# The order and the pacing of the indirect transfers that serve expert tiles beside an attention stage

## The reference

```python
xn = layernorm(x)
# attention
scores = einsum('bhqd,bhkd->bhqk', q, k) / sqrt(16) - slope[h] * |i - j|
s = (softmax(scores) @ v) @ W_out.T + b_out
# feed-forward: the 2 best of 8 experts per token, and a shared one
y = einsum('tei,eih->teh', silu(x @ w_gate) * (x @ w_up), w_down)
g = silu(einsum('teh,te->th', y, comb) + shared)
x = x + s * g
```

## Time and profile before

| | before |
|---|---|
| median of 3 runs | 1693.5 us (1691.61 to 1699.25) |
| profiled execution, its own time | 1699.23 us |
| span of its record | 1697.4 us, so 1.8 us lie around it |
| TensorE, ScalarE, VectorE, GpSimd busy | 90%, 78%, 60%, 29% of the span |
| granted clock of TensorE, mean | 0.975 of full speed |
| expert tiles on TensorE | from 496.0 us (first) to 1471.7 us (last turn) |

### The profile page before, as it was taken

One profiled execution on the slowest core, in us unless ns is written; L12 is line 12 of the kernel. 1 busy time (PEld: TensorE's weight loads), 2 busy tenths in 40 slices (PEclk: granted clock), 3 DMA queues, 4 the chain that ended last, 5 costly groups with the idle time before them and its releaser, 6 DMA issues. The chain is left out here.

```text
span 1697.4 us, 39816 instructions
## 1 busy us (share of the span) xinstructions
PE 1532.4 (90%) x15326; PEld 683.3 (40%) x15328; DVE 1012.4 (60%) x2738; ACT 1316.4 (78%) x1694; POOL 498.6 (29%) x477
## 2 busy tenths in 40 slices
PE   5998998889989999988999999989999999988896
PEld 3555564223334433333444333434443333322364
DVE  7788766988844444445444444454444444568776
ACT  5788777888878888877887878768888888788811
POOL 1222331000023333333443333333333333222143
PEclk9999998999999999999999999989999999999999
DMA  6858775233354454445454444445444454377795
GB/s 204 275 189 262 259 228 156 64 110 89 88 159 139 134 135 134 129 128 133 132 139 121 132 140 135 129 118 139 133 129 129 134 132 132 102 212 216 237 328 175
DMA packets 201087, 265.57 MB, mean 156 GB/s; under 512 B 90960, under 2 KB 158592, under 8 KB 200640
## 3 DMA queue, kind: packets, MB, share of 16 engines
q1 hardware_dynamic: 168256, 171.72, 36.1%
q0 software_dynamic: 24192, 82.86, 15.9%
q10 hardware_dynamic: 8448, 8.39, 1.4%
HBM read 180.56 MB, written 90.46 MB: 160 GB/s over the span
## 5 line engine op out<-in xcount | busy, mean ns | idle before, releaser
L1494 ACT ACTIVATE probs_att<-SC_att 128x1024 f32<-128x1024 f32 (+10 forms) x1306 | 1074.6, 912 | 209.3 <-PE SC_att L1377 179.5
L1403 PE MATMUL O_att<-probs_att,V_att 128*32 128x512 f32 (+7 forms) x8144 | 649.2, 414 | 61.1 <-DVE probs_att L1519 27.2
L1519 DVE TENSOR_TENSOR probs_att<-probs_att,decay 128x128 f32<-128x128 f32 x1024 | 265.7, 287 | 289.5 <-ACT probs_att L1494 246.9
L1403 PEld LDWEIGHTS O_att<-probs_att,V_att 128*32 128x32 f32 x8144 | 180.3, 111 | 221.0 <-issue 145.0
L1334 POOL DMA_INDIRECT ys<-ys_att,back_of_att x144 | 148.2, 1029 | 379.8 <-DVE ys_att L1585 272.1
L1377 PE MATMUL SC_att<-Q,K_turned_att 64*128 64x512 f16 (+7 forms) x1244 | 222.4, 310 | 15.7 <-ACT probs_att L1494 6.8
L1377 PE MATMUL SC_att<-Q,K 64*128 64x512 f16 (+9 forms) x1154 | 201.8, 303 | 10.3 <-DVE K_turned_att L1506 4.9
L1328 POOL DMA_INDIRECT x<-xn,row_of_att x144 | 139.5, 969 | 129.0 <-ACT probs_att L1494 98.2
L1322 POOL DMA_INDIRECT x<-w_rows,owner x72 | 74.0, 1028 | 346.8 <-DVE row_of_att L1568 215.2
L1377 PEld LDWEIGHTS SC_att<-Q,K_turned_att 64*128 64x128 f16 x1244 | 67.4, 94 | 266.3 <-ACT probs_att L1494 159.0
L699 POOL TENSOR_TENSOR inverse<-qk_tok,inverse 128x512 f16<-128x512 f32 x64 | 75.6, 1188 | 169.5 <-ACT inverse L731 162.6
(11 more groups left out here) (210 smaller groups left out, 1672.7 us busy)
## 6 DMA issues: line engine op xcount, KB each, us to landing
K<-k_stack SPq DMA_DIRECT2D x86, 256.0 KB
Q<-q_stack SPq DMA_DIRECT2D x86, 256.0 KB
x<-ys POOLq DMA_DIRECT2D x32, 512.0 KB, 4.8
x<-in_x SPq DMA_DIRECT2D x24, 512.0 KB, 7.2
k_stack<-inverse SPq DMA_DIRECT2D x96, 128.0 KB
q_stack<-inverse SPq DMA_DIRECT2D x96, 128.0 KB
inverse<-k_stack SPq DMA_DIRECT2D x42, 256.0 KB
inverse<-q_stack SPq DMA_DIRECT2D x42, 256.0 KB
```

The costliest lines, as they stand in the source:

```text
L1403: mm = pe.matmul(O[VW * g:VW * (g + 1), col:col + width * len(mine)], V[par][:, k, :], spans[:, j0:j0 + BPB * (len(mine) - 1) + 1:BPB, :], ...
L1494: nc.scalar.activation(probs[home][:, side + chunk.base:side + chunk.base + chunk.width], SC[:, c % SLOTS, start:start + chunk.width], ACT ...
L1519: v.tensor_tensor(diag, diag, decay[:, head_of(chunk.head), :], ALU.mult).then_inc(faded, 1)
```

## The change

The same 360 transfers (72 of weights, 144 of rows, 144 of results) are issued, with the same sizes, buffers and data semaphores. Two things differ.

The order: before, GpSimd goes through w(i+2), x0(i+2), x1(i+2), y0(i), y1(i) for each tile i. Now it goes through y0(i-1), x0(i+2), y1(i-1), x1(i+2), w(i+2). The results of a tile go out one tile later in the order, and the weights come last, not first.

The pace: before, the loads wait for 1500, 3300 and 5100 columns behind "turn" of tile i, the stores for 1500 and 3300 columns behind "down" of tile i. Now all five are counted from "turn" of tile i: 500, 2800, 5100, 7400 and 9700 columns, so 2300 apart. The last tile's results wait for no count. The first two tiles' loads are unpaced, as before.

```diff
-PACE_W, PACE_XS, PACE_YS = 1500, (3300, 5100), (1500, 3300)
+PACE_YS, PACE_XS, PACE_W = (500, 5100), (2800, 7400), 9700
...
-                def load_tile(i):
+                def load_weights(i):
                     if i > 2:
                         pool.wait_ge(ff_down, i - 2)
                     if i > 1:
                         pool.wait_ge(expd, after("turn", i - 2, PACE_W))
                     nc.gpsimd.indirect_dma_start(w[:, i % 3, :], ...)
+
+                def load_rows(i, t):
                     if i > 1:
                         pool.wait_ge(ff_turned, i - 1)
-                    for t in range(2):
-                        if i > 1:
-                            pool.wait_ge(expd, after("turn", i - 2, PACE_XS[t]))
-                        nc.gpsimd.indirect_dma_start(xs[:, i % 2, t, :], ...)
-
-                def store_tile(i):
+                        pool.wait_ge(expd, after("turn", i - 2, PACE_XS[t]))
+                    nc.gpsimd.indirect_dma_start(xs[:, i % 2, t, :], ...)
+
+                def store_rows(i, t):
                     pool.wait_ge(ff_y, i + 1)
-                    for t in range(2):
-                        pool.wait_ge(expd, after("down", i, PACE_YS[t]))
-                        nc.gpsimd.indirect_dma_start(keep["ys"], ...)
+                    if i + 1 < TILES_IN:
+                        pool.wait_ge(expd, after("turn", i + 1, PACE_YS[t]))
+                    nc.gpsimd.indirect_dma_start(keep["ys"], ...)
...
                 for i in range(TILES_IN):
+                    for t in range(2):
+                        if i > 0:
+                            store_rows(i - 1, t)
+                        if i + 2 < TILES_IN:
+                            load_rows(i + 2, t)
                     if i + 2 < TILES_IN:
-                        load_tile(i + 2)
-                    store_tile(i)
+                        load_weights(i + 2)
+                for t in range(2):
+                    store_rows(TILES_IN - 1, t)
```

More of the change, by code:

```diff
@@ L1322, in load_tile @@
                     nc.gpsimd.indirect_dma_start(w[:, i % 3, :], None, keep["w_rows"], index(keep["owner"][:, i:i + 1])).then_inc(w_in[i % 3], 16)
+                def load_rows(i, t):
                     if i > 1:
                         pool.wait_ge(ff_turned, i - 1)
-                    for t in range(2):
-                        if i > 1:
-                            pool.wait_ge(expd, after("turn", i - 2, PACE_XS[t]))
-                        nc.gpsimd.indirect_dma_start(xs[:, i % 2, t, :], None, keep["xn"], index(row_of[:, t, i:i + 1])).then_inc(xs_in[i % 2], 16)
-                def store_tile(i):
+                        pool.wait_ge(expd, after("turn", i - 2, PACE_XS[t]))
+                    nc.gpsimd.indirect_dma_start(xs[:, i % 2, t, :], None, keep["xn"], index(row_of[:, t, i:i + 1])).then_inc(xs_in[i % 2], 16)
+                def store_rows(i, t):
                     pool.wait_ge(ff_y, i + 1)
-                    for t in range(2):
-                        pool.wait_ge(expd, after("down", i, PACE_YS[t]))
-                        nc.gpsimd.indirect_dma_start(keep["ys"], index(back_of[:, t, i:i + 1]), ys[:, i % 2, t, :], None).then_inc(ys_out[i % 2], 16)
+                    if i + 1 < TILES_IN:
+                        pool.wait_ge(expd, after("turn", i + 1, PACE_YS[t]))
+                    nc.gpsimd.indirect_dma_start(keep["ys"], index(back_of[:, t, i:i + 1]), ys[:, i % 2, t, :], None).then_inc(ys_out[i % 2], 16)
                 def fetch(j):
@@ L1345, in _ @@
                 pool.wait_ge(order_ready, 1)
-                load_tile(0)
-                load_tile(1)
+                for i in range(2):
+                    load_weights(i)
+                    for t in range(2):
+                        load_rows(i, t)
                 for i in range(TILES_IN):
+                    for t in range(2):
[3 more added lines that the diff above has]
+                            load_rows(i + 2, t)
                     if i + 2 < TILES_IN:
-                        load_tile(i + 2)
-                    store_tile(i)
+                        load_weights(i + 2)
+                for t in range(2):
+                    store_rows(TILES_IN - 1, t)
                 for n in range(2):
```

## The result

The changed kernel took 1672.35 us in the median (1668.55 to 1676.03, 4 runs), the kernel before, beside it on the same chip, 1692.55 us (1687.52 to 1699.25, 4 runs). The ratio is 0.9887, with a 95% interval from 0.9863 to 0.9912.

The account below looks back on a forecast made before the run. TensorE (93% busy) and ScalarE, passing chunks through three PSUM slots, bound the tiles' stretch. All terms were 0, sum 0: 1693.5 us against the median; 8-in-10 range 1681 to 1702 us.

Parts of the forecast that it names:

- The moved loads and stores cost nothing: Tiles' stretch: moved transfers still land before turn, gate or result's copy needs them, 15.5 to 18.4 us to spare; worth 0.
- The narrowest margin: Narrowest case the plan allows, two tiles of 10,112 columns and a "down" 4,032 behind the turn: 9.7 us left.
- GpSimd's waits change from VectorE's to exponentials', at no cost: GpSimd's queue in the tiles' stretch: its 243.6 us of waiting for VectorE turn into waits for exponentials; worth 0.
- the end of the tiles stays: Behind the last tile: same copy releases the last store, fetch still leaves near 1484.8 us; worth 0.
- What the trace doesn't show ... I take 0: Tiles' stretch: whether an indirect transfer under way slows other engines; bounded from -31 to +35 us, taken as 0.
- a sign that the prediction itself named for being wrong: Tiles' stretch: TensorE's unexplained waits and its half-clock stretches cut to less than half, with a shorter time.
- The dismissal of the gap at 741 to 744 us: Longest TensorE gap, 3.45 us before 743.99: claimed TensorE partly at work with records missing, so weak support for bunches costing.
- first rival: Tiles' stretch: bunched loads keep DMA engines from something TensorE needs, so spreading gains; 1678 us, chance 0.16.
- Half of its bound: Size taken for bunches costing in the tiles' stretch: half of 31 us, giving 1678 us.
- The second rival: VectorE's fades and turning of K: GpSimd's spread issues hold them, up to 100 ns each; +18 us, 1711 us, chance 0.11.
- the 832 ns of K's turning: VectorE's longest turning of K, cited against GpSimd's issues holding VectorE, which would need one of over 1 us.
- It doesn't do what it says: GpSimd's issues: rounding to chunks brings transfers together again, so nothing changes, as in the forecast; no separate chance given.

Follow-up runs that it names:

- e2: Changed kernel, spacing still even, but weights issued first and the other transfers at other places in the tile; ratio 0.9893 to the kernel before.
- e4: Changed kernel's even spacing with the order of the kernel before (weights, rows, rows, result, result); ratio 0.9893 to the kernel before.
- e1: Changed kernel with all five counts at 5100 columns, so a tile's five transfers are issued back to back; 1796.23 us, ratio 1.0623 to before.
- e5: Bunched as e1, but each load moves only 64 bytes per partition, with the same number of issues; ratio 1.0676 to the kernel before.
- e8: Bunched as e1 with the same bytes, but loads are plain transfers from a fixed place, stores still indirect; ratio 0.9772 to the kernel before.
- e3: Changed kernel, still spread, but each load moves only 64 bytes per partition, with the same number of issues; ratio 0.9880 to the kernel before.
- e9: As e8, with the stores of 64 tiles made plain transfers to fixed places too; ratio 0.9752 to the kernel before.
- e10: As e8, with GpSimd filling each load's target with zeros ahead of the plain load; ratio 0.9770 to the kernel before.
- e11: As e1, with each indirect load fetching 64 rows instead of 128; ratio 1.0826 to the kernel before.

## Why the prediction was wrong, step by step

**The moved loads and stores cost nothing: right.** No wait before a turn, a gate or a result's copy was ended by a transfer, and e2 and e4 put the transfers elsewhere for the same time. (The narrowest margin, 9.7 us, leaves out the 3.7 us of TensorE's lead that the other three hold; it is 6.0.)

**GpSimd's waits change from VectorE's to exponentials', at no cost; the end of the tiles stays: right.** 198.7 us of waits before stores are for exponentials now, and behind the last tile the comparison by exponentials moves by 2 us only.

**"What the trace doesn't show ... I take 0": the step that failed.** The term was bounded from -31 to +35 us, and the measured -20 lies inside. I chose 0 because fades keep their median, "285 stands 14 ns from the minimum of 271". That row answers another question: how long an instruction takes once it has started. The fades' median is 285 ns in e1 too; what changes is when TensorE starts the next matmul and when a finished score reaches ScalarE. The rows for that were in the profile: ScalarE's waits for scores that had been done, and TensorE's 15.3 us without a recorded cause, whose fall to less than half, with a shorter time, is part of a sign that the prediction itself named for being wrong. The second of these rows needs care. At 743.99 TensorE starts 0.1 us behind the end of VectorE's copy (743.20 and 0.69 us), for which it waits; only the record of that signal is missing, and it was the copy that came late. Of all TensorE's waits of this kind between 505 and 1410 us, 21.2 us, 17.3 end within 0.16 us of the end of an instruction of VectorE or ScalarE. Most of them are time lost further down the chain, not holds of TensorE's own starts.

**The dismissal of the gap at 741 to 744 us: wrong.** "TensorE was at work in part of this gap and its records are missing" was the argument against the first rival. Every one of the 14 traces has 3560 score matmuls and 1306 exponentials, one for each chunk, and the page of the kernel before has 15326 matmuls beside 15328 weight loads, so by that count two matmuls are missing in the whole kernel. "Remote" says only that no recorded instruction ended shortly before the semaphore rose. VectorE's copy waits there for a semaphore that TensorE's sums raise, and the last of them ended, as modelled, at 738.49, 4.7 us before. TensorE stood, right behind four indirect issues in a row.

**The first rival: right on the gain, wrong on the cause.** Half of its bound gave 1678 us; 1672 came out. The half was chosen and not worked out, so coming so near is partly luck. (Half way to 1678 would be 1686; the range's lower end, 1681, lies beyond that, and the result beyond both.) Its mechanism, loads that keep the DMA engines from something TensorE needs, falls with e5 (bytes gone, 1.0676) and e8 (bytes there, 0.9772). The Trainium skill (DMA: Bandwidth & Descriptors, "Issuing engines are not separate DMA queues") has all transfers interleave on the same 16 DMA engines; that may well be so, but no run here shows it to cost anything: e3 is no faster than the changed kernel. Nor do the transfers of instructions, which the rival names, go with the holds: between 505 and 1410 us the kernel before has 104 packets of them and e9, with one late score, 109; only 12 of the 56 late scores of the kernel before had one beside them.

**The second rival, VectorE held for the length of an issue: wrong.** Fades have a mean of 286 ns in the changed kernel, but an instruction that is held starts late and need not take longer, so neither that nor the 832 ns of K's turning, on which the prediction relied, tests it. The starts do: between 505 and 1410 us VectorE stood waiting for over 200 ns before 211 fades in the kernel before and before 211 in the changed one, and each of them began at most 102 ns behind the end of an exponential, 32 in the median. No turning of K stands in the lists of waits.

**"It doesn't do what it says": wrong**, though in part true: 46 of 360 issues are still close.

**What the runs put in its place.** While GpSimd issues an indirect transfer, TensorE's starts and its finished scores can be held. Over all 14 kernels 616 of the 619 late scores have their modelled end within 1.5 us behind the start of an indirect issue (where 807 others were on time), and of the 1320 waits whose scores ended elsewhere 3 were late. The more issues, the later the score: where one indirect issue started between 1.5 us before the score's end and the exponential, late scores are 0.8 us late in the median and 1.8 at most; with two of them 1.6 and 3.3, with four 4.7 and 5.5. A longer wait meets more issues by itself, so these figures fit the account and do not prove it. By it TensorE's lead over ScalarE mostly covers one hold. A second issue 1.3 us later begins before the first hold is over, so the holds of a row join, the lead runs out, ScalarE waits, TensorE then lacks exponentials, and its clock falls (0.94 in e1's stretch against 0.99). That is why the cost grows faster than the number of close issues: from 46 of them to 142 the time grows by 1.1% of before, from 142 to 282 by 6.2%. It is shown that the indirect issue on GpSimd is the cause (e5, e8, e9, e10) and the spacing the lever (e1, e2, e4). What in the issue holds TensorE, its instructions or its completions first, stays open: a late score and a late start look alike where TensorE's ends are modelled.

## What to carry to other kernels

Where GpSimd issues indirect transfers beside a busy TensorE, space them out (2.8 us from one to the next was enough here, 1.4 was not, and nothing between was tried), and make every one plain whose rows lie behind one another, with the first row read into a register. To see whether it matters, look for waits of ScalarE on scores that were long done, or for TensorE's waits without a recorded cause, and set their times against GpSimd's issues, not against the DMA engines' load. Unchanged durations are no evidence that engines don't disturb one another: starts have to be looked at too. And a wait that ends on "issue" or "remote" need not lack a cause: look whose end lies right before it, or whose signal is due.

## What was not expected of the hardware

- Behind rows of five indirect issues finished scores came up to 6.1 us late (e1), and the kernel was 6 to 8% slower (e1, e5, e11), in e5 with the DMA engines at 9% in the worst stretch.
- A plain transfer issued by GpSimd, same queue, same packets, takes it 0.55 us instead of 1.0 and holds nothing that can be seen (e8, e9). Fills by GpSimd hold nothing that shows in the time either (e10).
- An indirect issue takes 0.91 us for 64 rows (e11) and 0.97 for 128 (e1), in the median of the row loads: nearly all of it is there whatever the number of rows.
- The Trainium skill (SBUF — State Buffer, "Who interferes with whom") says of the ports to that memory that TensorE and ScalarE never wait on another engine. e10 agrees: with 2.03 us of fills among GpSimd's 5.65 us of work in 6.96 (two of 0.69 us and one of 0.65), TensorE is 99% busy. For indirect issues the measurement decides: there TensorE does stand, by whatever way.
